# VectorE's tile table: four plain words a tile and one four-register load, and the two waits ahead of the first pass exchanged

## The reference

```python
def _displace(x, offset):            # x here is the group-normalised input
    off_px = offset * 64.0
    off_int = jnp.round(off_px)      # whole pixels, one pair per position, 48 positions
    sub = off_px - off_int           # the rest sets the 3x3 kernel
    ...                              # shifted[y, x] = x[y - dy, x - dx], 0 outside
    kern = jnp.exp(-(kx * kx + ky * ky) / (2.0 * 0.5 * 0.5))
    kern = kern / kern.sum(axis=(1, 2), keepdims=True)
    return lax.conv_general_dilated(shifted, ..., feature_group_count=C)

x = x + _displace(_gn(x, G=32), offset)
```

## Time and profile before

| | |
|---|---|
| median of 3 runs | 1061.57 us (1060.87 to 1061.63) |
| the profiled execution's own time | 1058.16 us |
| its span in the trace | 1055.9 us, 2.3 us less than its time |
| VectorE busy | 835.4 us, 79% |
| TensorE busy | 831.7 us, 79% |
| ScalarE busy | 649.9 us, 62% |
| GpSimd busy | 374.6 us, 35% |
| share of the 16 DMA engines taken by packets | 92.3% |
| moved | 403.08 MB, 382 GB/s in the mean |

### The profile page before, as it was taken

How to read it: one execution, slowest core, us unless ns; L and a number is a source line. 1 busy time by engine, 2 the same in 40 slices (tenths; PEclk the granted TensorE clock), 3 DMA queues, 4 the chain that set the end, 5 groups by cost and what they waited for, 6 DMA issues and landing times.

```text
span 1055.9 us, 9775 instructions
## 1 busy us (share of the span) xinstructions
PE 831.7 (79%) x2176; PEld 393.1 (37%) x2176; DVE 835.4 (79%) x567; ACT 649.9 (62%) x547; POOL 374.6 (35%) x332
## 2 busy tenths in 40 slices
PE   5985887878888798778789888888987988798710
PEld 2442333334333344333434344434443434344310
DVE  8198797987958788796887969796888969678685
ACT  0675556665567674677566576665655676685761
POOL 3034412634222424243733222332434426324221
PEclk9998898998988899889889989989999889889955
DMA  9827998999999899989999999999999999999937
GB/s 368 350 110 272 416 395 336 423 359 431 376 400 431 322 429 390 406 366 394 421 354 426 423 429 432 429 429 432 429 407 423 377 411 385 402 427 428 390 139 302
DMA packets 27820, 403.08 MB, mean 382 GB/s; under 512 B 3216, under 2 KB 3216, under 8 KB 3216
## 3 DMA queue, kind: packets, MB, share of 16 engines
q1 hardware_dynamic: 27792, 402.71, 92.3%
HBM read 201.38 MB, written 201.33 MB: 381 GB/s over the span
## 4 chain that ended last, share of the span: by engine, by line
DVE 36%; DMA 23%; PE 22%; issue 6%; POOL 5%; ACT 5%; DVEq 2%; ACTq 1%; SPq 0%; POOLq 0%
PE sum_ps L246 19%; DMA xs<-x_dram 19%; DVE xs L527 8%; DVE xs L530 8%; DVE xs L533 7%; DVE smooth L523 6%; DVE smooth L518 6%; DMA out_dram<-xs 4%; ACT frame L320 3%; POOL small L212 2%; POOL small L216 2%; ACTq L298 1%; ACT sum_ps L336 0%; POOL small L224 0%; POOL small L219 0%
## 5 line engine op out<-in xcount | busy, mean ns | idle before, releaser
L246 PE MATMUL sum_ps<-xs,bands 128*128 128x512 f32 x1024 | 505.9, 652 | 49.4 <-DMA xs<-x_dram 49.4
L352 ACT ACTIVATE unused<-xs,small 128x4096 bf16 (+1 forms) x96 | 356.1, 3709 | 17.9 <-ACT small L341 7.6
L246 PEld LDWEIGHTS sum_ps<-xs,bands 128*128 128x128 f32 x1024 | 208.3, 209 | 298.3 <-issue 280.6
L320 ACT ACTIVATE frame<-xs,small (+1 forms) x96 | 223.3, 2327 | 153.5 <-DVE smooth L523 151.9
L246 PE MATMUL sum_ps<-xs,halves 128*128 128x512 f32 x512 | 253.8, 653 | 75.5 <-DMA xs<-x_dram 75.5
L518 DVE SCALAR_TENSOR_TENSOR smooth<-frame,xs 128x1700 f32 (+5 forms) x96 | 163.7, 1705 | 160.3 <-ACT frame L330 104.8
L212 POOL TENSOR_TENSOR small<-small 128x3 f32<-128x3 f32 x32 | 60.2, 1882 | 638.7 <-ACT small L360 638.7
L527 DVE SCALAR_TENSOR_TENSOR xs<-smooth,small,xs 128x1700 f32 (+5 forms) x96 | 163.6, 1704 | 33.4 <-POOL small L224 30.6
L246 PEld LDWEIGHTS sum_ps<-xs,halves 128*128 128x128 f32 x512 | 105.0, 209 | 223.0 <-issue 126.8
L523 DVE SCALAR_TENSOR_TENSOR smooth<-frame,xs,smooth 128x1700 f32<-128x1700 f32 (+5 forms) x96 | 163.5, 1703 | 9.6 <-DVE smooth L518 5.3
L530 DVE SCALAR_TENSOR_TENSOR xs<-smooth,small,xs 128x594 f32 (+9 forms) x96 | 159.8, 1665 | 3.4
(11 more groups left out here) (81 smaller groups left out, 258.5 us busy)
## 6 DMA issues: line engine op xcount, KB each, us to landing
xs<-x_dram SPq DMA_DIRECT2D x96, 2048.0 KB, 14.8
out_dram<-xs SPq DMA_DIRECT2D x96, 2048.0 KB, 13.6
smooth<-offset_dram SPq DMA_DIRECT2D x1, 48.0 KB, 4.1
```

Of the source, the lines that this page charges most:

```text
L246: last = nc.tensor.matmul(sum_ps[:, :], (FIRST, SAME, SECOND)[i], slot_px(n, c * BANK, (c + 1) * BANK), start=(i == 0 and c == 0), stop=(i ...
L320: nc.scalar.activation(frame[:, bass.ds(b, rows * PITCH)].rearrange("p (r c) -> p r c", c=PITCH)[:, :, LEFT:LEFT + W], xs[:, bass.ds(a, ro ...
L352: nc.scalar.activation(unused[:, :], xs[:, bass.ds(n % SLOTS * PIX, PIX)], ACT.Square, bias=neg_mean[:, i:i + 1], accum_out=squares[:, i:i ...
```

## The change

The packed word is replaced by four words a tile in the table `words`: KIND (the form), TO (the place in `xs`, the slot's base included), FROM (the place in `frame`) and COLUMN (where the tile's weights stand in `col_w`). One `reg_load` with four registers brings them in at the same place in the stream as the one-word load before. The shifts and masks that took the word apart, and the two remainders that counted slot and column, are gone; four `snap`s of the loaded registers stand in their place.

In `smooth_tile` the two waits ahead of pass 1 are exchanged. Before, the wait for the last pass of the tile before (`tile_done`) stood alone in the stream and pass 1 itself carried the wait for `frame_ready`. Now the wait for `frame_ready` stands alone and pass 1 carries the one for `tile_done`.

Ahead of the loop GpSimd has 16 more small memsets before the one of `frame` (nine for the slots' bases, six for the columns, one for the table's last entry). VectorE's packing of the table has five instructions in place of nine, and the last of them waits for `zeros_ready`.

```diff
+    WORDS = 4
+    KIND, TO, FROM, COLUMN = range(WORDS)
...
-        windows = sb("windows", [P, TILES + 1], i32)
+        words = sb("words", [P, WORDS * (TILES + 1)], i32)
...
+            for s in range(SLOTS):
+                V.memset(slot_of.rearrange("p (n s) -> p n s", s=SLOTS)[:, :, s], float(s * PIX))
+            for i in range(2 * UT):
+                V.memset(word_of[:, :, COLUMN].rearrange("p (u i) -> p u i", i=2 * UT)[:, :, i], 3 * i)
+
+            V.memset(words[:, WORDS * TILES:], 0)
...
-            V.tensor_scalar(parts[:, KIND], edge[:, :, 0], -1.0, float(len(SIDES) ** 2 - 1), ALU.mult, ALU.add)
-            V.scalar_tensor_tensor(parts[:, TO], start[:, :, 1], float(W), start[:, :, 0], ALU.mult, ALU.add)
-            chained(V.scalar_tensor_tensor(edge[:, :, 1], window[:, :, 1], float(PITCH), window[:, :, 0],
+            chained(V.tensor_scalar(word_of[:, :, KIND], edge[:, :, 0], -1.0, float(len(SIDES) ** 2 - 1),
+                                    ALU.mult, ALU.add))
+            chained(V.scalar_tensor_tensor(edge[:, :, 1], start[:, :, 1], float(W), start[:, :, 0],
                                            ALU.mult, ALU.add))
-            chained(V.tensor_scalar(parts[:, FROM], edge[:, :, 1], float(PAD * PITCH + LEFT), None, ALU.add))
-            V.tensor_scalar(parts[:, TO], parts[:, TO], FROM_BITS, None, ALU.logical_shift_left)
-            chained(V.tensor_scalar(parts[:, KIND], parts[:, KIND], FROM_BITS + TO_BITS, None,
-                                    ALU.logical_shift_left))
-            chained(V.tensor_tensor(windows[:, 0:TILES], parts[:, KIND], parts[:, TO], ALU.bitwise_or))
-            V.tensor_copy(windows[:, TILES:], parts[:, FROM, 0:1])
-            chained(V.tensor_tensor(windows[:, 0:TILES], windows[:, 0:TILES], parts[:, FROM], ALU.bitwise_or))
+            chained(V.scalar_tensor_tensor(edge[:, :, 0], window[:, :, 1], float(PITCH), window[:, :, 0],
+                                           ALU.mult, ALU.add))
+            chained(V.tensor_scalar(word_of[:, :, FROM], edge[:, :, 0], float(PAD * PITCH + LEFT), None, ALU.add))
+            dve.wait_ge(zeros_ready, 1)
+            chained(V.tensor_tensor(word_of[:, :, TO], edge[:, :, 1], slot_of[:, 0:TILES], ALU.add))
...
-                dve.wait_ge(tile_done, done)
+                dve.wait_ge(frame_ready, done)
                 V.scalar_tensor_tensor(sm, frame_window(-1), side_w[:, bass.ds(n, 1), 0], frame_window(0),
                                        ALU.mult, ALU.add
-                                       ).wait_op(frame_ready, done_count, "sem-ge").then_inc(half_smooth, 1)
-
-                dve.reg_load(entry, windows[0:1, bass.ds(done, 1)])
+                                       ).wait_op(tile_done, done_count, "sem-ge").then_inc(half_smooth, 1)
+
+                dve.reg_load(next_tile, words[0:1, bass.ds(done * WORDS, WORDS)])
...
-                dve.reg_mov(column, n % (2 * UT) * 3)
-                weights = dve.snap(column, min_val=0, max_val=(2 * UT - 1) * 3)
-                word = dve.snap(entry, min_val=0, max_val=(len(SIDES) ** 2 << FROM_BITS + TO_BITS) - 1)
-                kind_of = dve.snap(word >> FROM_BITS + TO_BITS)
-                base = dve.snap(slot, min_val=0, max_val=(SLOTS - 1) * PIX)
-                dve.reg_mov(to_pixel, base + ((word >> FROM_BITS) & (1 << TO_BITS) - 1))
-                dst = dve.snap(to_pixel, min_val=0, max_val=SLOTS * PIX)
-                dve.reg_mov(from_pixel, word & (1 << FROM_BITS) - 1)
-                src = dve.snap(from_pixel, min_val=1, max_val=FRAME_ROWS * PITCH)
-                dve.reg_mov(slot, (base + PIX) % (SLOTS * PIX))
+                kind_of = dve.snap(next_tile[KIND], min_val=0, max_val=len(SIDES) ** 2 - 1)
+                dst = dve.snap(next_tile[TO], min_val=0, max_val=SLOTS * PIX)
+                src = dve.snap(next_tile[FROM], min_val=1, max_val=FRAME_ROWS * PITCH)
+                weights = dve.snap(next_tile[COLUMN], min_val=0, max_val=(2 * UT - 1) * 3)
```

More of the change, by code:

```diff
@@ L53, in of_tile @@
         return tiles[block * UT + n % UT, half]
-    TO_BITS = ((H - SIDES[-1]) * (W + 1)).bit_length()
-    FROM_BITS = (FRAME_ROWS * PITCH).bit_length()
+    WORDS = 4
+    KIND, TO, FROM, COLUMN = range(WORDS)
     EDGE_BITS = (PITCH - 1).bit_length()
@@ L107, in build @@
         e = setup[:, 7:10]
-        parts = smooth[:, 26 * TILES:29 * TILES].bitcast(i32).rearrange("p (n f) -> p n f", n=3)
+        TURNS = TILES // SLOTS + 1
+        slot_of = smooth[:, 26 * TILES:26 * TILES + TURNS * SLOTS]
+        word_of = words[:, 0:WORDS * TILES].rearrange("p (n k) -> p n k", k=WORDS)
         given = smooth[:, 21 * TILES:21 * TILES + 2 * POSITIONS].rearrange("p (f a) -> p f a", a=2)
@@ L463, in _ @@
                                            edge[:, :, 0], ALU.mult, ALU.add))
-            KIND, TO, FROM = range(3)
             chained(V.scalar_tensor_tensor(edge[:, :, 0], kind[:, :, 1], float(len(SIDES)), kind[:, :, 0],
                                            ALU.mult, ALU.add))
-            V.tensor_scalar(parts[:, KIND], edge[:, :, 0], -1.0, float(len(SIDES) ** 2 - 1), ALU.mult, ALU.add)
-            V.scalar_tensor_tensor(parts[:, TO], start[:, :, 1], float(W), start[:, :, 0], ALU.mult, ALU.add)
-            chained(V.scalar_tensor_tensor(edge[:, :, 1], window[:, :, 1], float(PITCH), window[:, :, 0],
+            chained(V.tensor_scalar(word_of[:, :, KIND], edge[:, :, 0], -1.0, float(len(SIDES) ** 2 - 1),
+                                    ALU.mult, ALU.add))
+            chained(V.scalar_tensor_tensor(edge[:, :, 1], start[:, :, 1], float(W), start[:, :, 0],
                                            ALU.mult, ALU.add))
-            chained(V.tensor_scalar(parts[:, FROM], edge[:, :, 1], float(PAD * PITCH + LEFT), None, ALU.add))
-            V.tensor_scalar(parts[:, TO], parts[:, TO], FROM_BITS, None, ALU.logical_shift_left)
-            chained(V.tensor_scalar(parts[:, KIND], parts[:, KIND], FROM_BITS + TO_BITS, None,
-                                    ALU.logical_shift_left))
-            chained(V.tensor_tensor(windows[:, 0:TILES], parts[:, KIND], parts[:, TO], ALU.bitwise_or))
-            V.tensor_copy(windows[:, TILES:], parts[:, FROM, 0:1])
-            chained(V.tensor_tensor(windows[:, 0:TILES], windows[:, 0:TILES], parts[:, FROM], ALU.bitwise_or))
+            chained(V.scalar_tensor_tensor(edge[:, :, 0], window[:, :, 1], float(PITCH), window[:, :, 0],
[3 more added lines that the diff above has]
+            chained(V.tensor_tensor(word_of[:, :, TO], edge[:, :, 1], slot_of[:, 0:TILES], ALU.add))
             dve.wait_ge(exps_ready, 1)
@@ L495, in _ @@
             V.engine_nop().then_inc(tile_done, 1)
[L497 to L500, removed]
+            next_tile = [dve.alloc_register(name) for name in ("next_kind", "next_to", "next_from", "next_column")]
             done_count = dve.alloc_register("done_count")
-            column = dve.alloc_register("column")
             def smooth_tile(rows, cols, src, dst, n, done, weights):
@@ L559, in tile_of @@
                 choose(dve, kind_of, 0, len(SIDES) ** 2, emit)
-            dve.reg_mov(slot, 0)
-            dve.reg_load(entry, windows[0:1, 0:1])
+            dve.reg_load(next_tile, words[0:1, 0:WORDS])
             dve.addr_align(256, max_nops=0)
```

## The result

| | before | after |
|---|---|---|
| median | 1061.57 us (1060.63 to 1065.18, 5 runs) | 1052.81 us (1051.96 to 1055.05, 5 runs) |
| the profiled execution's own time | 1058.16 us | 1052.22 us |
| its span | 1055.9 us | 1050.0 us |

The ratio is 0.9917, with a 95% interval from 0.9895 to 0.9938: faster by 0.8%. That is 8.8 us between the medians and 5.9 us between the profiled executions. The forecast was 1059.3 us with a range from 1054.3 to 1063.7.

The account below looks back on a forecast made before the run. No engine fills the span; VectorE savings were taken to count only where the DMA engines are not full. Early boundaries -6.0, late frames +2.0, load +1.7 gave -2.3 us: 1059.3 us, range 1054.3 to 1063.7.

Parts of the forecast that it names:

- The path: VectorE's sequencer work from pass 5 to the next pass 1: 0.8 us shorter, from 2.2 to 2.8 to 1.4 to 2.0.
- The boundaries with an early frame: Tile boundaries where the frame is ready before pass 5 ends: wait ahead of pass 1 becomes 0.04 us; together 6.0 us saved.
- the full stretch: 560 to 820 us, DMA engines full: five chain boundaries, 2.9 us, counted at nothing as covered.
- The late frame: Pass 1 behind a late frame starts 0.28 us later; seven such on the chain, 2.0 us lost.
- the fourth rival: The frame's wait becomes the bound: 0.28 us at each of 31 boundaries, +4.4 us, 1066.0 us; chance 0.07.
- The load of four words: Between passes 1 and 2: load 0.45 us longer than for one word, 1.7 us exposed on the chain.
- the cases with dearer words: Load rivals: further words cost 0.6 to 0.92 us (chance 0.15), or each is slow as its first, 1066.5 us or more (0.08).
- the eleven boundaries: Chain boundaries outside 560 to 820 us with long pass 5: idle ahead of pass 1 from 0.30 to 0.04, 3.0 us saved.
- the two with a pass 5 near 1.96 us: Boundary at 62.59 and a later one: the wait ahead of pass 1 falls to 0.04 us, together 1.2 us saved.
- the one at 495.73: Tile whose frame released it only 0.5 us before it began: may win 0.2 us.
- the rival of the full stretch: The gain passes through 560 to 820 us too: 2.9 us more saved, 1056.4 us, at the ends 1054.3; chance 0.15.
- The setup: Work ahead of the loop: `zeros_ready` 0.6 to 1.6 us after 9.00, at most 0.2 us on TensorE's start; counted at nothing.

Follow-up runs that it names:

- e9: The change plus three unread VectorE sums ahead of pass 1 at 12 short-tile boundaries off the chain: 1053.11 us, 0.9920 of the kernel before.
- e14: The change plus the same three sums ahead of pass 1 at 24 long tiles among 12 to 47: 1060.97 us, 0.9997 of the kernel before.
- e11: The change plus three unread VectorE sums ahead of pass 1 of tiles 0 to 11: 1058.33 us, 0.9968 of the kernel before.
- e13: The change plus three unread VectorE sums ahead of pass 1 of tiles 72 to 95: 1057.95 us, 0.9967 of the kernel before.
- e10: The change plus three unread VectorE sums ahead of pass 1 of tiles 48 to 71: 1055.69 us, 0.9948 of the kernel before.
- the repeat: The changed kernel run once more, unaltered: 1051.76 us, 0.9922 of the kernel before.
- e15: The change with one Newton step of GpSimd's weights left out and the four-word load moved behind pass 3: 1048.76 us, 0.9887 of the kernel before.

## Why the prediction was wrong, and where it was right

**The path** was right: 0.8 us forecast, 0.8 at 1030.59, which is the 0.71 and the head's 0.09. I had charged 0.12 for the snaps, which took nothing, and had credited 0.2 to the head, which gave 0.09. That the two errors cancel is luck.

**The boundaries with an early frame** became 0.04 us as forecast. e9 and e14 show that counting them on the chain was the right way, and e11 and e13 do not contradict it. e10 gives no leave to drop those of the full stretch.

**The late frame** costs 0.28 us as forecast, but I kept the chain of before for the count. After, four such boundaries are on the first chain and not seven, which makes 1.1 us in place of 2.0, but eleven are on the repeat's. The size of this term is open. The faster VectorE does wait for frames more often (41 times, against 31 and 37 in the two traces of before), as the fourth rival said, and the kernel did not become slower by it.

**The load of four words is the step that failed.** The prediction put its exposed part at 1.7 us, by a load 0.45 us longer. Its median is 0.035 us longer, and VectorE's waits ahead of pass 2 are 6.3 us in all after, against 6.4. The term is nought. The figure of the Trainium skill that the prediction quoted ("Runtime: NRT & Kernel Launch", section "Instruction fetch mechanics"), some 200 ns for each register, is not borne out for these loads: by it the load would take an estimated 0.93 us, and the row has 0.36. These loads read SBUF. I had put 0.23 on the cases with dearer words.

**The full stretch is a second term that had no sufficient reason.** Five boundaries on the chain, 2.9 us, were put at nothing because the DMA share there was 1.01. e10 does not bear that out: its cost fits four such boundaries at full price, and does not exclude that they are partly covered. Whether the 2.9 us were saved is open. For it: with the load at nothing, the late frames at four and the 2.9 us in full, the sum below is -8.1 us, near the 7.7 measured. Against it: from pass 1 of tile 48 to that of tile 72 the two traces of before take 239.6 and 241.2 us and the three of the change 239.5, 240.3 and 240.7, so nothing like 2.9 us was saved there. By the sign that the prediction named, a shorter stretch, the rival is not confirmed.

**The sum with these sizes**, on the terms of the forecast: the eleven boundaries 3.0 us, the two with a pass 5 near 1.96 us 1.2, the last two tiles 0.8 each (1.18 to 0.39, 1.70 to 0.88) and the one at 495.73, now 490.55, 0.5 (1.41 to 0.93), together -6.3; late frames +1.1, load 0, the full stretch 0: -5.2 us. The first two profiled executions are 5.9 us apart. This sum was put together after the result, with the early boundaries of one chain and the late frames of another, so its nearness proves little. The profiled executions of before (1058.16 and 1059.64 us) and of the change (1052.22, 1051.76 and 1050.91) give anything from 5.9 to 8.7 us, with 7.3 between their means.

The range reached down by the rival of the full stretch alone (without it to 1057.2), and its upper end, 1063.7, follows from no term that the prediction gives.

**What stays open** is the rest of 2.5 us to the measured 7.7 (three ratios), or of 3.6 us to the 8.8 between the medians of the first pair. The full stretch would fill most of it. I had also added the same 3.4 us on both sides to come from the profiled execution to the median. For before it was 3.4 and 1.1 us in its two measurements, for the change 0.6, 0.0 and 3.3: that is scatter, and part of the 8.8 us is too. The table alone has 5.6 us where the chain would give it about 2.8, with an interval that reaches down to 3.0. Boundaries outside the chain that count are neither found nor excluded, except in e9's place.

**The setup** counted at nothing, and nothing is seen of it. `zeros_ready` came 0.7 us later, inside the forecast.

**The signs.** The path, the idle of 0.04 us and the 0.28 us behind a late frame came as named, and pass 2 waited at 14 tiles, more than ten. The load did not come near 0.8 us, and the DMA share from 62 to 560 us hardly rose (0.93 in both, 377 and 382 GB/s).

## What to carry to other kernels

Register work between two instructions of an engine costs what the instruction ahead of it is too short to cover; measure it from the start of the one to the start of the next, and count first the boundaries on the chain, which can be tested by adding real work there. Read from the trace by how much that work lengthens the boundary before you reckon with it, and take the chains of several executions, for nearly equal paths change places. Put the wait that usually ends last on the instruction itself and the other ahead of it, and bring all registers with one load. When an engine's holes close, look at once for who was using them, and make the count of the new waits on new chains, not on the old one. Full DMA engines are no proof that time on the chain is covered.

## What was not expected of the hardware

- A load of four neighbouring words into registers takes 363 ns in the median, a load of one word 328 ns. Four one-word loads one after another take 2.9 us together.
- A load takes either about 0.3 us or about 0.9, before and after alike (39 and 41 of the 96 in the loop over 0.45 us). Behind pass 3 (e15) 68 of 96 took the longer time, and of ScalarE's single words 70 before and 65 after. No run here says why.
- Three small sums of 0.41 us each on VectorE delay the next pass by 0.86 us, since they overlap with each other and with the passes around them.
- Closing holes of 0.3 to 0.7 us on VectorE made GpSimd's small operations longer on the whole: its busy time rose from 374.6 to 412.0 us, and pass 3's waits for the weights grew by 16 us.
